# One DMA transpose for both half floats of a softmax tile, and the rotation's third swap issued before the fourth tile's transpose

## What is computed

```python
xn = _layernorm(x)
x = x + attn(xn) + ffn(xn)

# attn: its own layer norm, then 16 heads of 128
q = rope(x @ wq.T + bq);  k = rope(x @ wk.T + bk);  v = x @ wv.T + bv
# rope(t) = t * cos + rotate_half(t) * sin
attn = softmax(where(causal, -inf, q @ k.T / sqrt(128)))
return (attn @ v) @ wo.T + bo + residual

# ffn: sigmoid gate, 4 of 32 experts for each token, capacity 2 * (256 * 4 / 32) = 64
#      rows for an expert, silu(x @ w1) * (x @ w3) @ w2, and one shared expert
```

## Time and profile before

| | |
|---|---|
| median of three executions | 1086.97 us |
| profiled execution, its own time | 1084.02 us |
| span of its profile | 1082.2 us |
| TensorE busy | 923.4 us, 85% |
| VectorE busy | 750.9 us, 69% |
| ScalarE busy | 654.4 us, 60% |
| GpSimd busy | 771.5 us, 71% |
| SyncE's DMA queue | 63.9% of 16 engines' span |
| transposing DMAs | 256 of the high, 256 of the low halves |
| swaps | 256 DMAs of 128 KB |

### The profile page before, as it was taken

The page is one execution under the profiler, slowest core; times in us unless marked ns, Lnnn a source line. Parts: engine busy times, 40 slices in busy tenths (PEclk is TensorE's granted clock), DMA queues, the critical chain, the costliest instruction groups (busy, mean ns, idle before and its releaser), DMA issues.

```text
span 1082.2 us, 16885 instructions
## 1 busy us (share of the span) xinstructions
PE 923.4 (85%) x5341; PEld 719.2 (66%) x5341; DVE 750.9 (69%) x1695; ACT 654.4 (60%) x1326; POOL 771.5 (71%) x660
## 2 busy tenths in 40 slices
PE   8997878798978878787998989799898989979876
PEld 5785656575767666565776767677675767767655
DVE  8856657777787788766576567666676655766665
ACT  5676545566656665555565657556565665656652
POOL 4777656776766676667777787886878787687891
PEclk9998989999999999989999999999899999999988
DMA  7226679767776556667677687767668776676676
GB/s 240 56 59 119 139 148 178 142 121 126 134 140 118 114 109 122 131 105 145 133 155 163 141 156 155 178 123 150 145 148 172 146 166 126 146 146 135 126 172 150
DMA packets 362983, 150.85 MB, mean 139 GB/s; under 512 B 323600, under 2 KB 340368, under 8 KB 362768
## 3 DMA queue, kind: packets, MB, share of 16 engines
q1 hardware_dynamic: 357216, 142.96, 63.9%
q0 software_dynamic: 5392, 6.56, 4.1%
q10 hardware_dynamic: 288, 0.26, 0.1%
HBM read 33.94 MB, written 10.90 MB: 41 GB/s over the span
## 4 chain that ended last, share of the span: by engine, by line
DVE 28%; POOL 15%; ACT 15%; issue 14%; PE 14%; DMA 9%; SPq 5%; ACTq 0%; POOLq 0%; DVEq 0%
DVE ps L1587 8%; DVE halves L1596 8%; ACT halves L1047 8%; DMA qs<-qb 7%; PE ps L304 5%; POOL qb L1739 4%; POOL qs L1740 4%; PE ps L306 4%; PE ps L305 4%; POOL qb L1743 4%; ACT ps L1038 3%; SPq L715 3%; DVE acc L1637 2%; POOL q_l L1172 1%; DVE ol L1610 1%
## 5 line engine op out<-in xcount | busy, mean ns | idle before, releaser
L1596 DVE SCALAR_TENSOR_TENSOR halves<-ps,halves 128x128 f16<-128x128 f32 (+7 forms) x256 | 192.5, 755 | 233.2 <-ACT halves L1047 229.7
L1038 ACT ACTIVATE ps<-ps,nmax 128x128 f32<-128x128 f32 (+7 forms) x256 | 182.9, 715 | 254.1 <-DVE nmax L1587 249.7
L1739 POOL TENSOR_TENSOR qb<-qb,k_sb 128x512 f32<-128x512 f32 x128 | 168.8, 1319 | 229.8 <-DMA qs<-qb 229.3
L304 PE MATMUL ps<-k_h,q_h 128*128 128x512 f32 (+3 forms) x384 | 144.2, 376 | 95.1 <-DVE halves L1596 52.9
L1587 DVE CUSTOM_DVE_ANT_0 ps<-ps,maskr 128x128 f32<-128x128 f32 (+7 forms) x256 | 192.6, 759 | 9.4 <-PE ps L306 8.9
L1743 POOL TENSOR_TENSOR qb<-qb,qs 128x512 f32<-128x512 f32 x128 | 166.7, 1302 | 18.3
L1740 POOL TENSOR_TENSOR qs<-qs,k_sb 128x512 f32<-128x512 f32 x128 | 169.0, 1321 | 0.0
L1047 ACT ACTIVATE halves<-ps 128x128 f16<-128x128 f32 (+7 forms) x256 | 165.6, 647 | 5.1 <-DMA pt_l<-halves 3.5
L304 PEld LDWEIGHTS ps<-k_h,q_h 128*128 128x128 f32 x384 | 74.2, 193 | 125.4 <-DVE halves L1596 74.2
L304 PE MATMUL ps<-pt_h,v_h 128*128 128x512 f16 (+3 forms) x390 | 131.6, 338 | 7.1 <-DMA pt_l<-halves 7.1
L306 PE MATMUL ps<-k_h,q_l 128*128 128x512 f32 (+3 forms) x384 | 134.2, 349 | 0.0
(11 more groups left out here) (200 smaller groups left out, 2141.8 us busy)
## 6 DMA issues: line engine op xcount, KB each, us to landing
qs<-qb SPq DMA_DIRECT2D x256, 128.0 KB
ew<-epack SPq DMA_DIRECT2D x16, 768.0 KB
rqk<-wqk SPq DMA_DIRECT2D x16, 256.0 KB, 3.5
pt_h<-halves SPq DMA_TRANSPOSE x256
pt_l<-halves SPq DMA_TRANSPOSE x256
rv<-wvp SPq DMA_DIRECT2D x8, 256.0 KB, 3.8
ro<-wop SPq DMA_DIRECT2D x16, 128.0 KB, 2.9
token_table<-xn SPq DMA_DIRECT2D x4, 512.0 KB, 4.4
```

What stands on the lines that cost most here:

```text
L304: eng.matmul(dst, lhs[0], rhs[0], start=start, stop=False)
L1038: act.activation(tile[t], tile[t], ACT.Exp, bias=nmax[:, t:t + 1], scale=-1.0, accum_out=rsum[:, t:t + 1]).then_inc(exp_done, 1)
L1596: dve.scalar_tensor_tensor(out=h[:, 1, 0:(t + 1) * P], in0=tile[t], scalar=PSCALE, in1=h[:, 0, 0:(t + 1) * P], op0=ALU.mult, op1=ALU.subtr ...
L1739: pool.tensor_tensor(qb[:, i, :], qb[:, i, :], cos_sb[:, c], ALU.mult).then_inc(rope_a, 1)
```

## The change

`halves` and `pt` get one more dimension, so that the high and the low half of each block of 128 keys lie side by side. `turn` then waits for `lo_done` alone and issues one transposing DMA of 2(t + 1) blocks in place of two of (t + 1). The counts on `turned` go from 32 to 16 a tile. In SyncE's order `swap(n+1, 2)` moves from behind `turn(n, 3)` to ahead of it. The instructions of ScalarE, VectorE and TensorE that touch the tiles keep their number and size and get another stride.

```diff
-        halves = [sb(f"halves{b}", [P, 2, (b + 5) * P], F16) for b in range(GT)]
+        halves = [sb(f"halves{b}", [P, b + 5, 2, P], F16) for b in range(GT)]
-        pt = [[sb(f"pt{c}_{s}", [P, GT, 4 * (c + 1), P], F16) for s in "hl"] for c in range(2)]
+        pt = [sb(f"pt{c}", [P, GT, 4 * (c + 1), 2, P], F16) for c in range(2)]
...
-                    pe.wait_ge(turned[b], 32 * (2 * u + c + 1))
+                    pe.wait_ge(turned[b], 16 * (2 * u + c + 1))
-                                [pt[c][i][:, a:GT, j, :] for i in range(2)], j == 0, j == 4 * c + 3)
+                                [pt[c][:, a:GT, j, i, :] for i in range(2)], j == 0, j == 4 * c + 3)
...
-            for i, done in enumerate((hi_done, lo_done)):
-                sp.wait_ge(done, TILES * n + t + 1)
-                sp.dma_start_transpose(pt[t // GT][i][:, t % GT, 0:t + 1, :],
-                                       halves[t % GT][:, i, 0:(t + 1) * P]).then_inc(turned[t % GT], 16)
+            sp.wait_ge(lo_done, TILES * n + t + 1)
+            sp.dma_start_transpose(pt[t // GT][:, t % GT, 0:t + 1, :, :].rearrange("p j i q -> p (j i) q"),
+                                   halves[t % GT][:, 0:t + 1, :, :].rearrange("p j i k -> p (j i k)")).then_inc(turned[t % GT], 16)
...
-                for t in range(4):
-                    turn(sp, n, t)
+                turn(sp, n, 0)
+                turn(sp, n, 1)
+                turn(sp, n, 2)
                 swap(sp, n + 1, 2)
+                turn(sp, n, 3)
                 turn(sp, n, 4)
...
-                act.activation(halves[t % GT][:, 0, 0:(t + 1) * P], tile[t], ACT.Copy, scale=PSCALE).then_inc(hi_done, 1)
+                act.activation(halves[t % GT][:, 0:t + 1, 0, :], tile[t].rearrange("p (j k) -> p j k", k=P), ACT.Copy,
+                               scale=PSCALE).then_inc(hi_done, 1)
...
-                dve.scalar_tensor_tensor(out=h[:, 1, 0:(t + 1) * P], in0=tile[t], scalar=PSCALE, in1=h[:, 0, 0:(t + 1) * P],
-                                         op0=ALU.mult, op1=ALU.subtract).then_inc(lo_done, 1)
+                dve.scalar_tensor_tensor(out=h[:, 0:t + 1, 1, :], in0=tile[t].rearrange("p (j k) -> p j k", k=P), scalar=PSCALE,
+                                         in1=h[:, 0:t + 1, 0, :], op0=ALU.mult, op1=ALU.subtract).then_inc(lo_done, 1)
```

More of the change, by code:

```diff
@@ L462, in weighted_part @@
                 for b in (2 * h, 2 * h + 1):
-                    pe.wait_ge(turned[b], 32 * (2 * u + 2))
+                    pe.wait_ge(turned[b], 16 * (2 * u + 2))
                 pe.wait_ge(vl_done, 4 * (u // 2) + 4)
@@ L470, in weighted_part @@
                     ins = three(pe, bank[:, a * P:(2 * h + 2) * P].rearrange("p (a b) -> p a b", b=P),
-                                (v_h[:, j, d], v_l[:, j, d]), [pt[1][i][:, a:2 * h + 2, j, :] for i in range(2)],
+                                (v_h[:, j, d], v_l[:, j, d]), [pt[1][:, a:2 * h + 2, j, i, :] for i in range(2)],
                                 j == 0, j == last)
@@ L1045, in prob_hi @@
                 if n or t >= GT:
-                    act.wait_ge(turned[t % GT], 32 * (2 * n + t // GT))
-                act.activation(halves[t % GT][:, 0, 0:(t + 1) * P], tile[t], ACT.Copy, scale=PSCALE).then_inc(hi_done, 1)
+                    act.wait_ge(turned[t % GT], 16 * (2 * n + t // GT))
+                act.activation(halves[t % GT][:, 0:t + 1, 0, :], tile[t].rearrange("p (j k) -> p j k", k=P), ACT.Copy,
+                               scale=PSCALE).then_inc(hi_done, 1)
             def out_hi(u, c):
```

## The result

The changed kernel took 1110.96 us, the median of three executions (1110.86 to 1113.01), against 1086.97 before. The ratio is 1.0228, with a 95% interval of 1.0200 to 1.0256. I had predicted 1090.3 and a range of 1076 to 1099. The direction was right; the loss is 24 us where 3.3 were forecast, outside the range. The profiled execution took 1110.96 us; its span is 1109.2, that of before 1082.2.

What follows compares the result with a forecast made beforehand. The softmax loop (VectorE, ScalarE, TensorE) had 57% of the chain, with the rotation on the path in expert units. Terms: 12.2 - 6.2 - 0.8 - 1.5 = +3.7, less 0.4, +3.3 us: 1090.3 us, range 1076 to 1099.

Steps and rivals of the forecast that it cites:

- 12.2: Expert units in sum: 13.8 us for part 1 in 12 units, 2 for the other four, less 3.6 gained.
- -1.5: Unit 31: TensorE's 3.01 us wait for `turn(30, 7)` shrinks by 1.5 us, as loads go earlier.
- the sum's last deduction: 0.4 us taken off the sum of +3.7 for SyncE's other, smaller delays.
- Tile 7's delay: Expert units: part 1's swap lands 1.15 us later in 12 units, 13.8 us, plus 2 us for the other four.
- TensorE gets cold: In expert units joined waits lower TensorE's clock in eight to ten units, 0.7 us each: sum +13, 1100 us; chance 0.17.
- the joint gap: TensorE in expert units: moved wait and delay join, 1.26 us becomes 2.4, about 1.6 more where `scores(n, 4)` waited.
- the credit of 3.6 us in the expert units: Part 2's swap goes earlier, so ScalarE's idle time before parts 3 and 0 shrinks: 3.6 us gain, bounds 2 and 7.
- the early units, -6.2 and -0.8: Units 0 to 4: -6.2 us net from earlier issues; unit 13: the 0.8 us stall for `turn(12, 7)` goes.
- +1.3 for this place: Unit 3: another 2 MB transfer crowds tile 7 and part 1, a loss of 1.3 us.
- a missed path: Sign for the middle units: a change of over 0.5 us each would mean a path had been missed.
- The issue of 16 blocks: SyncE takes 1.4 us to issue one transpose of sixteen blocks, bounds 1.2 and 2.6.
- The rival of the doubled issue: If sixteen blocks take SyncE 2.6 us to issue, weights and part 1's swap go 1.2 us later: 1093 us; chance 0.07.

Runs made afterwards that it cites:

- e10: The kernel before with tile 7 alone turned in one transfer behind its low half; 1102.63 us, ratio 1.0194.
- e8: The changed kernel with ten matmuls on a constant ahead of `scores(n, 6)` in units 14 to 29; 1098.31 us, ratio 1.0145.
- e3: The changed kernel with tile 7 alone sent in two transfers, the high half as soon as ready; 1077.33 us, ratio 0.9916.
- e1: The kernel before with only the order changed, part 2's swap ahead of tile 3's two transposes; 1090.73 us, ratio 1.0058.
- e12: The changed kernel with GpSimd's 2 MB adding transfer issued in unit 8 in place of unit 3; 1107.63 us, ratio 1.0209.
- e14: e6 with GpSimd's 2 MB adding transfer cut into eight pieces, one in each of units 3 to 10; 1048.83 us, ratio 0.9658.
- e13: The kernel before with the same ten matmuls on a constant as e8, in units 14 to 29; 1088.87 us, ratio 1.0034.
- e11: The kernel before with tile 7's two transfers both issued only behind its low half; 1127.69 us, ratio 1.0401.
- e9: The kernel before, nothing merged, with part 2's swap ahead of tile 3's turn and the expert weights behind part 1's swap; 1069.29 us, ratio 0.9864.
- e6: The changed kernel with tile 7 alone in two transfers and the expert weights behind part 1's swap; 1056.59 us, ratio 0.9739.
- e7: The changed kernel with part 1's swap ahead of both tile 7's turn and the expert weights; 1136.61 us, ratio 1.0486.
- e5: The kernel before with the expert weights issued behind part 1's swap; 1088.73 us, ratio 1.0013.

## Why the prediction was wrong

**Where the miss lies.** The sum was +3.3 us, and the profiles are 27.0 apart. Of these 23.7 us, 13.6 are in the expert units (25.8 for 12.2), 9.2 ahead of unit 14 (2.2 for -7.0), 0.5 in the last two units (-1.0 for -1.5), and 0.4 is the sum's last deduction.

**Right.** The changed profile has 256 transposes. ScalarE's idle time before parts 0 and 3 nearly went (12.0 and 7.0 us in units 14 to 31 became 1.9 and 0). Part 2's swap went out 1.1 us behind its data on average in the expert units, in place of 6.9; "within 0.1 us" was too sharp. The swap of part 1 was to be in flight for about 6 us: 6.78 in unit 17. ScalarE's wait at queries was to rise to about 50 us: 55.5. Tile 7's delay alone was forecast at 13.8 + 2 = 15.8 us, and e10 measured 16.4. That this is so near is luck. It came out of another product, 1.03 us in all 16 units and not 1.15 in 12 and 2 us for the rest, and it holds an unknown part of the clock, for which the forecast had nothing. In the changed kernel the delay was 1.39 us in flight and 0.10 at the issue, and part 1's rounding had idle time in all 16 units, 67.2 us in place of 26.9.

**Wrong: the clock was put at nothing in the sum.** This is the largest step that failed. The rival "TensorE gets cold" had the mechanism, and its condition was met by the record's own numbers: the joint gap was put at 2.4 us and more, and the gap of the earlier trace rows that it was held against was 2.38. It still got no term and a chance of 0.17. The gap was 3.08 us in unit 17, and in 12 of the 16 units the clock fell. The filling of e8 gave back 9 us by the ratios and up to 13.7 in the profiles. The rival's price was 8 to 10 units at 0.7 us, some 6 us, a figure for which the record has no working. The 12 stretches are 51.2 us long and half of the clock is gone in them, so they lose up to 26 us; a third to a half of that reached the end.

**Wrong: the terms were added as if independent.** Tile 7's delay (16.4 alone) and the rest (-2.0 alone) add up to 14.4; together they made 25.8. The clock does not explain this excess of 11.4: above before, the stretches at the lower level are 27.3 us in e10 and 13.7 in e3, 41.0 together, and 44.4 in the changed kernel. ScalarE's idle time at all roundings of units 14 to 31 does show an excess: +18.5 us in e10, -5.4 in e3, and +21.6 in place of their sum of 13.1. The swap is part of it: its delay of 1.39 us is 0.39 more than those of e10 and e3 together (0.94 and 0.06), 6 us over 16 units. Why it is longer was not tested.

**Mis-sized: the credit of 3.6 us in the expert units.** It was given for idle time before part 3 and for unit 28's part 0. All parts but tile 7's merge brought 2.0 us (e3), the move alone 1.4 (e1). The idle time before part 3 went in both, and that before part 1's rounding rose from 28.9 us in units 14 to 31 to 42.9 (e3) and 41.3 (e1). What is gained at one arrival of a loop turns up as waiting at the latest one.

**Wrong: the early units, -6.2 and -0.8.** At the start of unit 3 the gain was 4.8 us (160.6 against 165.4), of 6.4 forecast for units 0 to 2. Then unit 3 took it back with 5.9. The record had +1.3 for this place. e12 and e14 show that the 2 MB transfer does it, and e13 that even the same instructions meet it in two ways. So this term had bounds of at least 6 us that one profile could not show. Units 4 to 13 lost 1.1 us more, with 1.9 in unit 7 alone, which is above the 0.5 us a unit that was to show a missed path; its cause was not tried.

**The issue of 16 blocks** was mis-sized: 1.4 us in the record, 2.01 in unit 17, median 1.93 for tile 7. It is not what cost: in e10 the same issue in unit 17 took 1.32 us and that of the weights 1.31 (0.91 in the changed kernel), so the time moves between the two, and the swap was issued within 0.13 us of its data on average in either. (The rival of the doubled issue has weights and swap go out 1.2 us later, and its +3 has no term for that.)

**The page's rules.** By "DMA: Bandwidth & Descriptors" of the Trainium skill, HWDGE ordering, a DMA engine takes its descriptors in ring order, and I noted that the expert units would cost 1.8 us more by it. The swap's delay of 1.39 us in flight in the changed kernel agrees with the 1.3 us of that reading; 1.55 in e11 is more, and 0.94 in e10 less. Its rule that small transfers should be coalesced agrees with tiles 0 to 6 (e9 against e6, 1.3%), and fails for tile 7, where coalescing means to wait for the later half with others queued behind.

What stays open: the 0.45 us between the swap's delays in e10 and in the changed kernel, and why e11, with no more data than the changed kernel, lost 8 us more in the expert units. Its trace has the swap 0.23 us later in all and the lower clock for 69.8 us in place of 51.2, which could cost 9 us at most; neither was tested by itself. Open as well is the clock's part in the losses of e10 and e7 and in the gain that e5 did not bring: of the kernels with long gaps only the changed one was filled.

## What to carry to other kernels

Before merging two transfers, ask when the first half used to leave, and who is queued behind the second: merge where SyncE's issue time is on the path, and keep apart the one whose data must be gone before a due transfer. When terms of a sum end at the same gap, don't add them: put them into one gap and look how long it becomes. If it reaches a length behind which the trace shows a lower clock, give the clock a term of its own, with all that the slow stretch can lose as its bound. Try moves in a shared queue in pairs: two that brought nothing alone brought 1.4% together here, and 3.4% with merges and a bulk transfer cut in pieces.

## What the hardware showed

In the changed kernel's expert units TensorE fell to its lower clock (granted 0.50) for 3.4 or 6.8 us at a time, behind idle gaps of 2.4 to 4.8 us, and useless matmuls in such gaps made the whole kernel 0.8% faster. There is no sharp length in these traces: in e10 gaps of 1.9 and 2.0 us (units 25 to 27) stood ahead of such stretches, in the changed kernel one of 2.3 us (unit 15) did not. A transpose from buffer to buffer takes SyncE 1.2 us for one block and 1.9 for sixteen by the median, but 7.77 beside a 2 MB transfer (8.06 in e12, in the unit to which the transfer was moved). The minimum, median and maximum in ns over all 256 of the changed kernel:

```profile
L714 SPq DMA_TRANSPOSE pt<-halves x256: 1185/1362/7773, 81.8 to 1096.9; - x128
```

A 2 MB transfer that no engine waits for at that time left all engines nearly idle for 10 us, with SyncE's transfers late beside it; in eight pieces it cost some 8 us less.
